# Value products of 400 columns in a cross-attention stage, with VectorE's work on outputs and reciprocals in another order

## The reference, cut to what matters

```python
# x: (8, 100, 512), context: (8, 361, 256); 16 query heads, 8 key/value heads, head size 128
x = x + tanh(g_xattn[0]) * xattn(layernorm(x), ctx, mask, Wq, Wk, Wv, Wo)
# xattn, for each batch b:
q = (text @ Wq)                  # 16 heads of 100 x 128
k, v = (ctx @ Wk), (ctx @ Wv)    # 8 heads of 361 x 128, each used by two query heads
scores = where(mask, q @ k.T / sqrt(128), -inf)
attn = softmax(scores)           # 100 x 361 for each query head
out = attn @ v                   # 100 x 128 for each query head
return out @ Wo
```

## Time and profile before

| | |
|---|---|
| three runs of the kernel before | 960.95, 961.73, 968.34 us, median 961.73 |
| the profiled execution | 965.36 us, span of its engines 963.6 us |
| TensorE's mean granted clock over the span | 0.974 of full speed |
| busy over the span | PE 94%, PEld 87%, DVE 66%, ACT 58%, POOL 41% |
| chain that ended last | PE 65%, DVE 14%, DMA 11%, ACT 4%, issue 4% |
| the cross-attention halves | about 61 to 213 us and 285 to 438 us of the span |

### The profile page before, as it was taken

One profiled execution on the slowest core, in us unless ns is written; L12 is line 12 of the kernel. 1 busy time (PEld: TensorE's weight loads), 2 busy tenths in 40 slices (PEclk: granted clock), 3 DMA queues, 4 the chain that ended last, 5 costly groups with the idle time before them and its releaser, 6 DMA issues.

```text
span 963.6 us, 16195 instructions
## 1 busy us (share of the span) xinstructions
PE 901.0 (94%) x5743; PEld 836.1 (87%) x5743; DVE 638.6 (66%) x1442; ACT 561.1 (58%) x1448; POOL 399.7 (41%) x384
## 2 busy tenths in 40 slices
PE   5999999999999999999989998799979999999997
PEld 4889999999999999999867767699979888988897
DVE  3557777743537777762486976575867778987764
ACT  3656666754546666663334767545446767776761
POOL 3432222345442223246534433344233766666531
PEclk9999999999999999999998899699999989999999
DMA  5734710016540000005431112134376989999876
GB/s 149 215 87 121 205 52 2 12 41 170 156 123 1 17 1 2 1 12 153 135 92 55 45 35 66 39 96 127 95 267 194 288 239 294 287 307 270 269 198 156
DMA packets 112760, 122.20 MB, mean 127 GB/s; under 512 B 9887, under 2 KB 77927, under 8 KB 112680
## 3 DMA queue, kind: packets, MB, share of 16 engines
q1 hardware_dynamic: 97806, 98.80, 33.2%
q0 software_dynamic: 5184, 12.13, 6.1%
q10 hardware_dynamic: 9690, 10.24, 3.7%
HBM read 110.72 MB, written 19.07 MB: 135 GB/s over the span
## 4 chain that ended last, share of the span: by engine, by line
PE 65%; DVE 14%; DMA 11%; ACT 4%; issue 4%; POOL 1%; ACTq 0%; SPq 0%; DVEq 0%; POOLq 0%
PE bank L2080 59%; PE bank L2209 4%; DVE we L1348 3%; DMA s_sum<-yo,target 2%; DMA eraw<-in_L_ffn_w_up_e_dram 2%; DMA eraw<-in_L_ffn_w_gate_e_dram 2%; DMA eraw<-in_L_ffn_w_down_e_dram 2%; DVE wf L1348 1%; DMA sums<-s_sum 1%; ACT we L921 1%; DMA raw<-in_L_xattn_Wq_dram 1%; DVE PQ L1345 1%; PE bank L2386 1%; POOL wx L1918 1%; DVE HDl L1348 1%
## 5 line engine op out<-in xcount | busy, mean ns | idle before, releaser
L1947 POOL TENSOR_SCALAR SC<-SC,mx,anyv 100x361 f32<-100x361 f32 x128 | 81.4, 647 | 211.5 <-DVE mx L1460 200.9
L1918 POOL TENSOR_TENSOR wf<-raw,wf 128x512 fp32r<-128x512 f32 x54 | 71.6, 1332 | 107.7 <-ACT wf L907 107.7
L1918 POOL TENSOR_TENSOR wx<-raw,wx 128x512 fp32r<-128x512 f32 x64 | 83.9, 1320 | 74.4 <-ACT wx L907 74.2
L921 ACT ACTIVATE we<-eraw 128x704 fp32r<-128x704 f32 (+2 forms) x140 | 96.1, 718 | 28.5 <-DMA eraw<-in_L_ffn_w_up_e_dram 8.8
L1348 DVE TENSOR_TENSOR we<-eraw,we 128x704 fp32r<-128x704 f32 (+2 forms) x100 | 92.2, 941 | 24.2 <-ACT we L921 23.9
L1930 POOL TENSOR_TENSOR we<-eraw,we 128x704 fp32r<-128x704 f32 x40 | 72.8, 1821 | 67.9 <-ACT we L921 67.7
L2080 PE MATMUL bank<-H2h,wf 128*128 128x400 f32 x352 | 99.0, 347 | 0.0
L1037 ACT ACTIVATE SC<-SC,mx 100x361 f32<-100x361 f32 x128 | 75.4, 593 | 29.1 <-DVE mx L1456 28.6
L2080 PE MATMUL bank<-XTh,wx 128*128 128x400 f32 x256 | 72.0, 354 | 3.3 <-POOL wx L1918 2.0
L1348 DVE TENSOR_TENSOR Kl<-bank,Kh 128x362 fp32r<-128x362 f32 x64 | 34.1, 534 | 60.3 <-ACT Kh L995 60.2
L1348 DVE TENSOR_TENSOR QOl<-bank,QOh 128x200 fp32r<-128x200 f32 (+1 forms) x96 | 41.4, 432 | 45.4 <-ACT QOh L950 35.4
(11 more groups left out here) (288 smaller groups left out, 2770.9 us busy)
## 6 DMA issues: line engine op xcount, KB each, us to landing
raw<-s_unit SPq DMA_DIRECT2D x60, 256.0 KB
eraw<-in_L_ffn_w_gate_e_dram SPq DMA_DIRECT2D x40, 352.0 KB
eraw<-in_L_ffn_w_up_e_dram SPq DMA_DIRECT2D x40, 352.0 KB
eraw<-in_L_ffn_w_down_e_dram SPq DMA_DIRECT2D x40, 256.0 KB
raw<-in_L_xattn_Wq_dram SPq DMA_DIRECT2D x32, 256.0 KB
raw<-in_L_xattn_Wo_dram SPq DMA_DIRECT2D x32, 256.0 KB
eraw<-in_L_ffn_w_down_e_dram SPq DMA_DIRECT2D x20, 192.0 KB
s_unit<-in_L_ffn_w_sh_gate_dram SPq DMA_DIRECT2D x11, 256.0 KB, 3.9
```

What stands on the lines that cost most here:

```text
L921: eng.activation(weights("e", u)[0:rows, 0, 0:n], eraw[u % 6][0:rows, 0:n], ACT.Copy).then_inc(sem("act_e"), 1)
L1918: eng.tensor_tensor(w[:, 1, :, :], raw[plan.raw[stream, u] % 4][:, :, :], f32(w[:, 0, :, :]), ALU.subtract).then_inc(sem("pool_w"), 1)
L1947: eng.tensor_scalar(sc, sc, m[:, 3, h:h + 1], anyv[:, b:b + 1], ALU.mult, ALU.mult).then_inc(sem("pool_p"), 1)
```

## The change

The high and low parts of the transposed probabilities get one tile (`PT`, for each chunk 200 columns high, then 200 columns low) instead of two. The value product of a chunk becomes two matmuls: the values' high part against all 400 columns, and the values' low part against the 200 high ones. Bank 7 then holds two results side by side: columns 0 to 199 the sum of high by high and low by high, columns 200 to 399 high by low. ScalarE copies the high part from the first 200 columns alone, as before; VectorE subtracts it (`low`), waits for its own result, and adds the second 200 columns in a further instruction. This `out_rest` comes one iteration later than the subtraction did (for step `i-4`), after the maxima and their scaling and before the low parts of the probabilities; the last one stands behind the loop. The reciprocals of step `i-1` come ahead of the maxima of step `i`. TensorE's waits are as they were.

```diff
-    PTh, PTl = [], []
-    for i in range(2):
-        PTh.append(A_.place(f"PTh{i}", [128, 3, 2 * T], R))
-        PTl.append(A_.place(f"PTl{i}", [128, 3, 2 * T], R))
+    PT = A_.ring("PT", 2, [128, 3, 2, 2 * T], R)
...
# ScalarE
-                    eng.activation(flat(PTh[t % 2][:, 0:2, :]), banks[5][:, 0:4 * T], ACT.Copy).then_inc(sem("act_pt"), 1)
+                    src = banks[5][:, 0:4 * T].rearrange("p (c q) -> p c q", c=2)
+                    eng.activation(PT[t % 2][:, 0:2, 0, :], src, ACT.Copy).then_inc(sem("act_pt"), 1)
...
# VectorE
+            def out_rest(i):
+                bo, go = steps[i]
+                t = half * NS + i
+                dve.wait_ge(sem("act_o"), t + 1)
+                main, rest = (banks[7][:, 2 * T * n:2 * T * (n + 1)].rearrange("p (h q) -> p h q", h=2) for n in range(2))
+                at = slice(2 * go, 2 * go + 2)
+                lo = QOl[:, at, batch_slice(bo)]
+                chained(low(lo, main, QOh[:, at, batch_slice(bo)]))
+                eng.tensor_tensor(lo, f32(lo), rest, ALU.add).then_inc(sem("dve_o"), 1)
...
+                if 1 <= i <= NS:
+                    t = half * NS + i - 1
+                    dve.wait_ge(sem("act_exp"), 2 * t + 2)
+                    eng.reciprocal(mx[t % 3][:, 3, :], mx[t % 3][:, 2, :]).then_inc(sem("dve_rec"), 1)
                 if live:
...
                     eng.tensor_scalar(m[:, 1, :], m[:, 0, :], -XS, None, ALU.mult).then_inc(sem("dve_nmx"), 1)
-                if 1 <= i <= NS:
-                    t = half * NS + i - 1
-                    dve.wait_ge(sem("act_exp"), 2 * t + 2)
-                    eng.reciprocal(mx[t % 3][:, 3, :], mx[t % 3][:, 2, :]).then_inc(sem("dve_rec"), 1)
+                if i >= 4:
+                    out_rest(i - 4)
...
-                if i >= 3:
-                    bo, go = steps[i - 3]
-                    t = half * NS + i - 3
-                    dve.wait_ge(sem("act_o"), t + 1)
-                    src = banks[7][:, 0:2 * T].rearrange("p (h q) -> p h q", h=2)
-                    at = slice(2 * go, 2 * go + 2)
-                    low(QOl[:, at, batch_slice(bo)], src, QOh[:, at, batch_slice(bo)]).then_inc(sem("dve_o"), 1)
...
+            out_rest(NS - 1)
...
# TensorE
-                    ph, pl = PTh[t % 2], PTl[t % 2]
+                    p = PT[t % 2]
                     for c, (_, n) in enumerate(CH):
-                        e = mm3(banks[7][:, 0:2 * T], Vh[0:n, c, gs], Vl[0:n, c, gs], ph[0:n, c, :], pl[0:n, c, :],
-                                c == 0, c == 2)
+                        mm(banks[7][:, 0:4 * T], Vh[0:n, c, gs], p[0:n, c, :, :], c == 0, False)
+                        e = mm(banks[7][:, 0:2 * T], Vl[0:n, c, gs], p[0:n, c, 0, :], False, c == 2)
                     e.then_inc(sem("pe_o"), 1)
```

More of the change, by code:

```diff
@@ L1027, in attention @@
                         act.wait_ge(sem("pe_o"), t - 1)
-                    eng.activation(flat(PTh[t % 2][:, 0:2, :]), banks[5][:, 0:4 * T], ACT.Copy).then_inc(sem("act_pt"), 1)
+                    src = banks[5][:, 0:4 * T].rearrange("p (c q) -> p c q", c=2)
+                    eng.activation(PT[t % 2][:, 0:2, 0, :], src, ACT.Copy).then_inc(sem("act_pt"), 1)
                     n = CH[2][1]
                     act.wait_ge(sem("pe_pt"), 2 * t + 2)
-                    eng.activation(PTh[t % 2][0:n, 2, :], banks[6][0:n, 0:2 * T], ACT.Copy).then_inc(sem("act_pt"), 1)
+                    eng.activation(PT[t % 2][0:n, 2, 0, :], banks[6][0:n, 0:2 * T], ACT.Copy).then_inc(sem("act_pt"), 1)
                 if live:
@@ L1464, in attention @@
                     dve.wait_ge(sem("act_pt"), 2 * t + 1)
-                    low(flat(PTl[t % 2][:, 0:2, :]), banks[5][:, 0:4 * T], flat(PTh[t % 2][:, 0:2, :])).then_inc(sem("dve_pt"), 1)
+                    src = banks[5][:, 0:4 * T].rearrange("p (c q) -> p c q", c=2)
+                    low(PT[t % 2][:, 0:2, 1, :], src, PT[t % 2][:, 0:2, 0, :]).then_inc(sem("dve_pt"), 1)
                     dve.wait_ge(sem("act_pt"), 2 * t + 2)
-                    low(PTl[t % 2][0:n, 2, :], banks[6][0:n, 0:2 * T], PTh[t % 2][0:n, 2, :]).then_inc(sem("dve_pt"), 1)
+                    low(PT[t % 2][0:n, 2, 1, :], banks[6][0:n, 0:2 * T], PT[t % 2][0:n, 2, 0, :]).then_inc(sem("dve_pt"), 1)
                 if live:
```

## The result

The changed kernel takes 984.67 us (median of 4 runs, 981.91 to 986.71) against 961.56 us (median of 4, 960.95 to 968.34): a ratio of 1.0234, with a 95% interval of 1.0185 to 1.0283. The forecast was 978, with a range of 965 to 988: slower, for the reason given, and by 23 us instead of 16.

What follows compares the result with a forecast made beforehand. TensorE's issue was taken as the bound; 24.5 us of new waits less 7.5 for wider matmuls and 1.0 for GpSimd gave +16.0 us, forecast 978 us, range 965 to 988.

Steps and rivals of the forecast that it cites:

- What bounds the kernel: Cross-attention: TensorE's issue is the bound, so a matmul saved is time saved and a new wait is lost in full.
- Part 1: Value product with wider matmuls: 0.87 us instead of 0.99 in each of 64 steps, saving 7.5 us.
- the forecast's own limit of 0.92: Test of the wider matmuls' saving: wrong if the product's six matmuls take over 0.92 us.
- rival D: Wide matmul saves only 2, waits at long end, or matmuls behind waits come slower: +27, 989 us; chance 0.16.
- Part 2: Reciprocals ahead of the maxima: GpSimd starts about 1.1 us earlier, gaining 1.0 of TensorE's 1.7 us of waits.
- Part 3: Output's low part behind the next maxima: TensorE's value product waits for bank 7, 28 waits, 24.5 us in both halves.
- S: Start of TensorE's first score matmul in a step, the zero from which maxima and product are timed.
- The chained wait: VectorE's addition after its subtraction: waiting for its own result costs 0.04 us, 0.38 apart, against the skill's rule.
- VectorE's load, "no bound": VectorE's own load: subtraction and addition fill the 0.88 us gap before the keys' low part, so no bound.
- A: Rival: bank 7 is read in time everywhere, the waits don't bite, the saving stands: 953 us; chance 0.06.
- B: Rival: waits at their short end, 18.1 us, saving of 9 and 1.7 for GpSimd: +7.4, 969 us; chance 0.16.
- C: The forecast itself: late maxima stop TensorE in 28 products, +16.0 us; chance 0.62.

Runs made afterwards that it cites:

- experiment 6: Kernel before with wide matmuls, output's subtraction and reciprocals at old places, addition and its wait left out: 956.89 us, ratio to before 0.9932.
- experiment 1: Changed kernel with the reciprocals back behind the scaling, all else as changed: 979.21 us, ratio to the kernel before 1.0171.
- experiment 8: Kernel before with the reciprocals ahead of the maxima, nothing else: 965.43 us, ratio to the kernel before 1.0011.
- experiment 3: Changed kernel without the addition, so the high values' product with the low probabilities is left out: 975.15 us, ratio to the kernel before 1.0126.
- experiment 4: Changed kernel with the output's subtraction and addition back at the end of their product's iteration: 982.23 us, ratio to the kernel before 1.0218.
- experiment 5: Kernel before with wide matmuls, output's subtraction and addition at the old place, reciprocals at theirs: 966.01 us, ratio to before 1.0014.
- experiment 7: Changed kernel with the output's subtraction and addition directly ahead of the same iteration's maxima: 976.67 us, ratio to the kernel before 1.0131.

## Why the forecast was right, and where its size was off

**What bounds the kernel.** Right: TensorE was full, and its new waits count in full: the halves are 21.65 us longer, each 10.8 where the forecast said 8. The sum of 16.0 falls 5.6 us short of that, mostly by two terms: the waits were put 3.1 us too low, and the saving 2.5 us too high. The forecast holds because its range was wide enough for both.

**Part 1, 7.5 us.** Right for a product that TensorE reaches without a stop: in the time line above a wide matmul and its narrow one take 0.30 us together (98.34 to 98.64), steps without waits are 0.12 us shorter, and experiment 6, where hardly any product waits, has 6.5 us at the end. Too large for the changed kernel, where 34 of 64 products start behind a stop and take 0.94 to 0.99 us, over the forecast's own limit of 0.92. The saving there is 5.0 us. That the matmuls behind a wait come slower at first stands in rival D and not in the sum.

**Part 2, a gain of 1.0 us.** Wrong in sign: the 1.7 us of waits for GpSimd went, and yet experiment 1, without the early reciprocals, is 4.3 us shorter in its halves. The reciprocals start GpSimd's two instructions so that they run across the scaling, and the scaling stands until the one under way ends. It is this step that failed: "GpSimd starts about 1.1 us earlier, and of the 1.7 us that TensorE waits for it I count 1.0 as gained". Experiments 1 and 8 and the rows of L1468 show it: 0.46 for 0.17 us, 0.27 us more from maximum to product at g = 6 behind contexts, g = 7 and i = 4. The Trainium skill (SBUF — State Buffer, section Who interferes with whom) says that VectorE and GpSimd share a pair of ports under a lock held for a whole instruction, that a `tensor_scalar` can need it, and that the second to come blocks. This trace agrees: the scaling ends at 97.35 and GpSimd at 97.33. It was not shown by a run of its own that these ports are the cause.

**Part 3, 24.5 us.** Right in mechanism and place, and nearly in count (30 waits for 28). The first maximum was met within 0.02 us where VectorE comes late to it (g = 6 behind contexts, 7, 0, i = 30); where the scores bind it, at g = 2 and i = 31, it is 0.83 us after S and not 0.72. From there to the product the terms were 0.1 us too large (1.91 measured where the scaling is undisturbed, 2.03 forecast, so the handoff and weight load cost about 0.05 rather than 0.17), and the scaling's 0.27 was missing. One wait was missed, g = 4 of each half's first batch (0.66), where the early steps all have value tiles and VectorE is late (the maximum 2.42 us after S, 1.49 before). Together 27.6 instead of 24.5. (Its low end should read 17.9, 24.5 less 20 x 0.25 and 8 x 0.20, and not 18.1; nothing hangs on it.)

**The chained wait.** The trace of after confirms 0.38 us from the subtraction to the addition (97.26 to 97.64); experiment 3 gives 0.39 for the whole instruction with its wait. The Trainium skill (VectorE: DVE Perf Modes, section The DRAIN you can't avoid) says that a chain of VectorE instructions takes no longer with a semaphore behind each; the measurement decides against it here: behind a subtraction of 0.35 us the next instruction starts 0.27 us after it without the wait, and 0.38 with it.

**VectorE's load, "no bound".** True of the changed kernel, where the addition lies in the idle time ahead of Kl, but the reason given was too coarse for its neighbours: at the old place the addition is in the round and does bind (experiments 4, 5 and 7). That also says what the new place buys: the addition out of the round, for a bank that is free too late.

**The rivals.** A (no waits) and B (short waits) are out by the distances. The measured 23 us lie between C (16) and D (27), and part of D's reason came true: the matmuls behind a wait did come slower at first. The rest, the stretched scaling, stands in no rival. The clock did not fall in the changed kernel (granted 1.00 throughout both halves), as forecast; once in experiment 4 it did.

## What to carry to other kernels

Before moving a read of an accumulator's bank to a later place in an engine's list, write down for each kind of step when the next writer comes to the bank and when the read would be done, from the same zero; the answer was within 0.15 us here in every kind but one, while shares of busy time say nothing about it. Idle time of an engine has sides: what fits into a wait is free, what stands elsewhere in the same round adds in full, so sum the round across engines, with the new instruction in it (here 37.3 us, 34.0 without it, against 36.4 of TensorE's), before calling it hidden. A saving read from a full stream holds for a full stream: if the same change makes the engine stop ahead of these matmuls, read what they take behind a stop too (0.96 us here instead of 0.86). And where VectorE and GpSimd both work in SBUF, starting GpSimd earlier can cost more than its lateness did.

## What the runs showed of the hardware that was not expected

A VectorE instruction of 100 x 2 elements took up to 0.60 us instead of 0.17 when a GpSimd instruction was under way. In the changed kernel 42 of 64 scalings are stretched, to between 0.25 and 0.60 us, and each of them ends 0.02 to 0.03 us after a GpSimd instruction does, so how long it lasts is only a matter of how early it started. It is one GpSimd instruction that it waits for, not GpSimd's whole work: a scaling in experiment 4 that began in the first of GpSimd's two ended with the first. Two scalings of the changed kernel that started only 0.10 us after a GpSimd instruction were not held at all (0.17 and 0.18 us); why is open. Over 64 scalings the median was 466 ns in experiment 4 and 169 in experiment 5. The maxima, which read PSUM, showed next to nothing of it (527 ns in the mean before, 529 after).

Behind a wait TensorE's first matmul of 400 columns started 0.05 to 0.06 us after VectorE's addition had ended (98.06, 104.22), and the next matmul followed it after about 0.29 us instead of 0.18.

The kernel before ran from 953.0 to 971.0 us over all measurements, and the granted clock of the whole span mostly goes with the time (0.984 at 953.0 us, 0.973 at 968.8). In the traces of all these kernels the clock is granted in full in the attention halves, but for the one fall told above, and the stretch between the halves lasts 72.5 to 73.8 us. What lies behind the second half, the same program in each, lasts 516.9 to 526.8 us, and there the granted clock of a stretch of 100 us or more goes down to 0.88. So most of the scatter lies there; what sets it was not looked into. Ratios of 0.5% need many runs of both kernels on this one.
